# Row maxima carried inside the attention's own contraction: three bf16 rows sent by SyncE transfers in place of the pick products

## The reference, cut to what matters

```python
q = x @ wq + bq                      # (256 rows, 16 heads, 8 wide)
s = q @ q.T / sqrt(128)              # per head, 256 x 256
p = softmax(s)                       # row maximum taken off first
y = (p @ q) @ wu + bu
```

## Time and profile before

| | |
|---|---|
| three timed runs | 2505.82, 2507.54 (median), 2507.85 us |
| the profiled execution's own time | 2515.66 us |
| its span, first to last instruction | 2513.9 us |
| TensorE matmuls busy | 2036.8 us (81%) |
| VectorE busy | 1426.1 us (57%) |
| ScalarE busy | 1236.0 us (49%) |
| GpSimd busy | 648.7 us (26%) |
| mean granted TensorE clock | 0.909 |

### The profile page before, as it was taken

One profiled execution on the slowest core, in us unless ns is written; L12 is line 12 of the kernel. 1 busy time (PEld: TensorE's weight loads), 2 busy tenths in 40 slices (PEclk: granted clock), 3 DMA queues, 4 the chain that ended last, 5 costly groups with the idle time before them and its releaser, 6 DMA issues.

```text
span 2513.9 us, 38918 instructions
## 1 busy us (share of the span) xinstructions
PE 2036.8 (81%) x13610; PEld 1594.7 (63%) x13610; DVE 1426.1 (57%) x4130; ACT 1236.0 (49%) x2670; POOL 648.7 (26%) x663
## 2 busy tenths in 40 slices
PE   2766773587878888998899889989998999788884
PEld 1555552476557556875787578757875886665764
DVE  5877536453556675566556565666566356356522
ACT  3766413444446455555555564555455446335431
POOL 3111003333131133124223322332233124013052
PEclk9777885699889899999899999999999999899997
DMA  7100000112211211312132213221322312312121
GB/s 237 43 1 1 1 1 0 31 45 64 56 47 44 65 52 57 85 55 55 52 91 57 65 39 89 62 65 32 92 67 60 88 52 68 89 29 61 41 62 47
DMA packets 228948, 141.29 MB, mean 56 GB/s; under 512 B 116489, under 2 KB 206732, under 8 KB 228754
## 3 DMA queue, kind: packets, MB, share of 16 engines
q1 hardware_dynamic: 174320, 85.60, 13.4%
q0 software_dynamic: 16960, 34.74, 4.6%
q10 hardware_dynamic: 37474, 18.46, 2.6%
HBM read 82.48 MB, written 57.16 MB: 56 GB/s over the span
## 4 chain that ended last, share of the span: by engine, by line
PE 53%; DVE 24%; ACT 12%; issue 6%; DMA 2%; POOL 2%; SPq 1%; ACTq 0%; POOLq 0%; DVEq 0%
PE PS L908 17%; PE PS L876 9%; DVE AR L1085 3%; PE PS L1207 3%; PE PS L1170 3%; PE PS L1188 3%; PE PS L1433 2%; PE PS L1193 2%; ACT AR L1141 2%; DVE small L332 2%; ACT AR L837 2%; ACT AR L362 2%; DVE AR L795 2%; DVE xnT L1269 1%; PE PS L911 1%
## 5 line engine op out<-in xcount | busy, mean ns | idle before, releaser
L908 PE MATMUL PS<-AR,W 128*128 128x256 f32 x2560 | 653.0, 404 | 20.9 <-DVE AR L795 15.0
L795 DVE TENSOR_TENSOR AR<-AR,PS 128x512 f32<-128x512 f32 (+1 forms) x384 | 228.6, 597 | 653.9 <-ACT AR L837 525.8
L908 PEld LDWEIGHTS PS<-AR,W 128*128 128x128 f32 x2560 | 499.8, 204 | 92.1 <-issue 17.0
L837 ACT ACTIVATE AR<-PS 128x512 f32<-128x512 f32 (+1 forms) x384 | 201.1, 525 | 556.5 <-PE PS L908 439.1
L1085 DVE TENSOR_REDUCE AR<-PS 128x2 f32<-128x512 f32 x512 | 337.2, 688 | 160.0 <-PE PS L1170 155.6
L1141 ACT ACTIVATE AR<-PS 128x512 f32<-128x512 f32 x512 | 303.6, 600 | 236.3 <-PE PS L1193 231.9
L876 PE MATMUL PS<-AR,WO 128*128 128x256 f32 (+1 forms) x1536 | 357.7, 383 | 0.0
L876 PEld LDWEIGHTS PS<-AR,WO 128*128 128x128 f32 (+1 forms) x1536 | 295.5, 193 | 42.8
L1170 PE MATMUL PS<-AR 128*128 128x256 bf16 x1024 | 204.8, 287 | 40.4 <-DVE AR L1085 25.9
L743 POOL DMA_INDIRECT AR<-YE,gidx1c x128 | 128.8, 1007 | 379.8 <-issue 231.4
L743 POOL DMA_INDIRECT AR<-YE,gidx x128 | 128.3, 1002 | 350.9 <-ACT AR L1141 310.8
(11 more groups left out here) (359 smaller groups left out, 2771.5 us busy)
## 6 DMA issues: line engine op xcount, KB each, us to landing
AR<-XE SPq DMA_DIRECT2D x128, 128.0 KB, 2.1
YE<-AR ACTq DMA_DIRECT2D x128, 128.0 KB
AR<-QD SPq DMA_DIRECT2D x384, 32.0 KB
QD<-AR SPq DMA_DIRECT2D x8, 768.0 KB, 5.2
AR<-KD SPq DMA_DIRECT2D x64, 96.0 KB
W<-in_L_ffn_w_kernel_dram SPq DMA_DIRECT2D x2, 2560.0 KB, 13.5
OD<-AR SPq DMA_DIRECT2D x128, 36.0 KB
X<-in_L_attn_dense_dram SPq DMA_DIRECT2D x8, 512.0 KB, 4.5
```

Of the source, the lines that this page charges most:

```text
L795: ins = dve.tensor_tensor(hf[:, cols], gl[i % 2][:, cols], H[:, 2 * (i % 2) + 1, cols], ALU.mult)
L837: ins = act.activation(gl[i % 2][:, cols], H[:, 2 * (i % 2), cols], ACT.Gelu_apprx_tanh)
L908: mm = pe.matmul(H[:, b0, b * CAP:(b + 1) * CAP], w0[:, e, hb * P:(hb + 1) * P], xeT[e % 2], start=True, stop=True)
```

## The change

The three negated bf16 parts of the maxima become rows 48 to 50 of the queries' tile QA, and rows 48 to 50 of the keys' tile KA hold ones, so that the two `shifted` products add the maxima by themselves and the two pick products go. To get there: VectorE writes the parts in an order that gives each slot three neighbouring rows; TensorE transposes them with two transposes instead of one; ScalarE copies 32 rows of 256 columns to MP; SyncE then moves MP to QA with eight transfers of three rows for each piece (`shifts`), and `shifted` waits at each piece's first slot for those transfers (`a_md`). The split moves to the slot in which the piece's last maximum is taken (slots 3, 8, 16, 24, ..., 48), the transposes and the copy to two slots after it (5, 10, 18, 26, 34, 42, 50), the values product behind that. Scores run up to 16 slots ahead instead of 14. The queries' loads go from six transfers to three, two of which repeat their source rows; the queries' image is written by three transfers instead of one. GpSimd issues five transfers more, once, in the first round.

```diff
-MROWS = 3 * 2 * PB
+MROWS = KR
 def scored(i):
-    return min(NS, i + PB + 6, PB + 2 * (i + 1))
+    return min(NS, i + 2 * PB, PB + 2 * (i + 1))
+SPLIT = [slot_of(PB * (c + 2) - 1) for c in range(NPC - 1)]
+TURN = [i + 2 for i in SPLIT]
+VALUES = [TURN[0] + 2] + [i + 3 for i in TURN[1:]]
 # load_kq
-for lo, hi, a in ((0, 8, 0), (8, 16, 0), (16, 24, 0), (24, 32, 8), (32, 40, 8), (40, 48, 16)):
-    sp.dma_start(QA[c % DEPTH][lo:hi, :], qr[a:a + hi - lo, :]).then_inc(S["a_kq%d" % (c % DEPTH)], 16)
+for lo, times, part in ((0, 3, 0), (3 * AD, 2, 1)):
+    rows = qr[part * AD:(part + 1) * AD].rearrange("(o d) t -> o d t", o=1)
+    sp.dma_start(QA[c % DEPTH][lo:lo + times * AD, :], rows.broadcast_to([times, AD, 2 * QUAD])
+                 ).then_inc(S["a_kq%d" % (c % DEPTH)], 16)
+sp.dma_start(QA[c % DEPTH][5 * AD:7 * AD, :], qr[2 * AD:4 * AD, :]
+             ).then_inc(S["a_kq%d" % (c % DEPTH)], 16)
 # afront_parts
-sp.dma_start(QD.rearrange("c a p t -> p (c a) t"), QP.rearrange("p c a t -> p (c a) t")
-             ).then_inc(S["a_qd"], 16)
+for a in range(3):
+    sp.dma_start(QD[:, a].rearrange("c p t -> p c t"), QP[:, :, a, :]).then_inc(S["a_qd"], 16)
 # attend_act, turned
-act.wait_ge(S["a_mxT"], NPC * n + c + 1)
-act.copy(MP[c % 2], turned_maxima(c)).then_inc(S["a_mp"], 1)
+k = NPC * n + c
+act.wait_ge(S["a_mxT"], k + 1)
+if k >= 2:
+    act.wait_ge(S["a_md"], 16 * PB * (k - 1))
+act.copy(MP[c % 2][0:32], turned_maxima(c)[0:32]).then_inc(S["a_mp"], 1)
 # attend_pe, maxima
-pe.transpose(turned_maxima(c), MS[c % 2].rearrange("p a b -> p (a b)"),
-             identb[:, :]).then_inc(S["a_mxT"], 1)
+for q in range(2):
+    mm = pe.transpose(turned_maxima(c)[:, q * P:(q + 1) * P], MS[c % 2][:, q, :], identb[:, :])
+mm.then_inc(S["a_mxT"], 1)
 # attend_pe, shifted
+if b == 0:
+    pe.wait_ge(S["a_md"], 16 * PB * (NPC * n + c + 1))
 for h in range(2):
-    pe.matmul(o[:, h * 256:(h + 1) * 256], keys(c, P, h, b), queries(c, b), start=(h == 0),
-              stop=False, skip_group_check=True)
-if b == 0:
-    pe.wait_ge(S["a_mp"], NPC * n + c + 1)
-for q in range(2):
-    mm = pe.matmul(o.rearrange("p (h q t) -> p q h t", h=2, q=2)[:, q],
-                   pick[:, q * PB + b:q * PB + b + 1].broadcast_to([P, P]),
-                   MP[c % 2].rearrange("p (o t) -> p o t", o=1).broadcast_to([P, 2, P]),
-                   start=False, stop=True, skip_group_check=True)
+    mm = pe.matmul(o[:, h * 256:(h + 1) * 256], keys(c, P, h, b), queries(c, b), start=True, stop=True)
 mm.then_inc(S["a_slot"], 1)
 # attend_sp
+def shifts(c):
+    sp.wait_ge(S["a_mp"], NPC * n + c + 1)
+    image = QA[c % DEPTH][MROWS:MROWS + 3, :].rearrange("p (g b t) -> p b g t", g=AH, b=PB)
+    for b in range(PB):
+        sp.dma_start(image[:, b], MP[c % 2][3 * b:3 * b + 3, :].rearrange("p (g t) -> p g t", g=AH)
+                     ).then_inc(S["a_md"], 16)
+
+if n is not None:
+    shifts(0)
 for c in range(NC):
     beside(c)
     if n is None:
         continue
     for p in (2 * c, 2 * c + 1):
+        if p + 1 < NPC:
+            shifts(p + 1)
         if p + DEPTH < NPC:
             sp.wait_ge(S["a_slot"], PB * (NPC * n + p + 1))
             load_kq(sp, n, p + DEPTH)
 # round_pool, first round
+for k in range(DEPTH):
+    pool.dma_start(KA[k].rearrange("p g (s t) -> p (g s) t", t=P)[MROWS:MROWS + 3],
+                   onesb[0:3, :].rearrange("p (o t) -> p o t", o=1).broadcast_to(
+                       [3, 2 * QUAD // P, P])).then_inc(S["a_kone"], 16)
+pool.dma_start(QD[:, 3].rearrange("c (u p) t -> c u (p t)", u=AD),
+               KA[0][HALF:P].rearrange("p g t -> p (g t)")).then_inc(S["a_kone"], 16)
```

More of the change, by code:

```diff
@@ L121, in build @@
         identb = sb("identb", [P, P], BF16)
-        pick = sb("pick", [P, 2 * PB], BF16)
         join = sb("join", [P, AD], BF16)
@@ L210, in build @@
         mrest = ar.take((2 * PB,))
-        MS = [ar.take((P // (2 * PB), 2 * PB), BF16) for _ in range(2)]
-        MP = [ar.take((P,), BF16) for _ in range(2)]
+        MS = [ar.take((2, P), BF16) for _ in range(2)]
+        MP = [ar.take((2 * P,), BF16) for _ in range(2)]
         qTf = tmp[:, :, :].rearrange("p a b -> p (a b)")
@@ L1068, in turned_maxima @@
         def turned_maxima(c):
-            return side_bank(c).bitcast(BF16)[:, 0:P]
+            return side_bank(c).bitcast(BF16)
         def attend_dve(dve, n, ch, beside):
@@ L1109, in attend_dve @@
                 done = scored(i)
[L1110 to L1114, removed]
+                if i in SPLIT:
+                    split(SPLIT.index(i) + 1)
+                if i in VALUES:
+                    values(VALUES.index(i) + 1)
         def attend_act(act, n, beside, stored=None):
@@ L1143, in attend_act @@
                     out(i // 16 if i % 16 > 4 else i // 16 - 1, (i // 4 - 1) % 4)
-                if li == 5 and c + 1 < NPC:
-                    turned(c + 1)
+                if i in TURN:
+                    turned(TURN.index(i) + 1)
             if n is not None:
@@ L1150, in values @@
             def values(c):
-                pe.wait_ge(S["a_mp"], NPC * n + max(c, 1))
+                pe.wait_ge(S["a_mp"], NPC * n + c + 1)
                 for b in range(PB):
@@ L1159, in scores @@
             def scores(c, b):
+                if b == 0 and c == 0 and n == 0:
+                    pe.wait_ge(S["a_kone"], 16 * (DEPTH + 1))
                 if b == 0:
-                    pe.wait_ge(S["a_kq%d" % (c % DEPTH)], 16 * 9 * (NPC // DEPTH * n + c // DEPTH + 1))
+                    pe.wait_ge(S["a_kq%d" % (c % DEPTH)], 16 * 6 * (NPC // DEPTH * n + c // DEPTH + 1))
                 if c >= 1:
@@ L1225, in attend_pe @@
                 shifted(i)
-                if c + 1 < NPC:
-                    if li == 2:
-                        if c == 0:
-                            pe.wait_ge(S["m_ysb"], stored)
-                        values(c + 1)
-                    if li == 5:
-                        maxima(c + 1)
+                if i in TURN:
+                    if i == TURN[0]:
+                        pe.wait_ge(S["m_ysb"], stored)
+                    maxima(TURN.index(i) + 1)
+                if i in VALUES:
+                    values(VALUES.index(i) + 1)
                 if li == 5:
@@ L2115, in lights @@
                     if R.has(-1):
-                        b.put((16, lambda: hold(act, S["a_qd"], 64 * (R.g(-1) + 1))),
+                        b.put((16, lambda: hold(act, S["a_qd"], 96 * (R.g(-1) + 1))),
                               (16, lambda: hold(act, S["a_kp"], 3 * (R.g(-1) + 1))))
@@ L2503, in _ @@
             ch.step(pool.memset(zrow, 0.0))
-            ch.step(pool.memset(pick[:, :], 0.0))
             ch.step(pool.memset(anti, 0.0))
@@ L2538, in _ @@
             ch.wait()
-            ch.step(pool.tensor_tensor(pick[0:MROWS, :], identb[0:MROWS, 0:2 * PB], identb[0:MROWS, 2 * PB:4 * PB],
-                                       ALU.add))
             ch.link(pool.tensor_tensor(join[0:3 * AD, :], identb[0:3 * AD, 0:AD], identb[0:3 * AD, AD:2 * AD],
                                        ALU.add))
-            ch.step(pool.tensor_tensor(pick[0:MROWS, :], pick[0:MROWS, :], identb[0:MROWS, 4 * PB:6 * PB], ALU.add))
             ch.link(pool.tensor_tensor(join[0:3 * AD, :], join[0:3 * AD, :], identb[0:3 * AD, 2 * AD:3 * AD],
```

17 lines of the change are left out of this document (9 added, 8 removed).

## The result

| | before | after |
|---|---|---|
| timed, median (lowest to highest) | 2507.69 us (2505.82 to 2516.18) | 2819.85 us (2817.44 to 2832.11) |
| ratio, with its 95% interval | | 1.125 (1.1221 to 1.1279) |
| span of the profiled execution | 2513.9 us | 2820.0 us |
| mean granted TensorE clock | 0.909 | 0.849 |
| time at the lower clock level, by the profile's record of the clock | 461 us | 856 us |

Slower, as forecast, but by 312 us where the forecast had 61.5. The time lies outside the range (to 2660) and also beyond the dear rival (a), 2699.

What follows compares the result with a forecast made beforehand. Inside an attention three engines were taken to share the limit. Terms -38 + 60 + 10 + 13 + 12 + 2.5 + 2 = +61.5 us on 2507.5 gave 2569 us; range for 8 in 10, 2525 to 2660.

Steps and rivals of the forecast that it cites:

- (a): Rival on SyncE's row transfers: 0.81 us from start to start, 130 us more in all, 2699 us; chance 0.17.
- slot 56: Piece 7's rows queue behind SyncE's wait for scatters: 8.6 us late in seven stages, +60 us; stage 0 +10 us.
- pieces 1 to 6: Waits for rows at these pieces' first slots, mostly hidden: 1.5 us a stage, +12 us in all.
- piece 0 of stage 1: Opening of stage 1: 1.5 us from copy to products where 4.1 are needed, +2.5 us.
- Part 2: Rows through SyncE: 512 transfers, 0.34 us from start to start, landing 1.7 us; MP ready to rows ready 4.1 us.
- The clock: TensorE at the lower clock after each stage's new stall: 1.6 us lost, eight times, +13 us.
- Part 3, "hidden" loads: Queries' loads issued nine slots before the scores need them: hidden; three fewer save SyncE 1.0 us a piece.
- Part 3, the lead at 0: Scores two slots further ahead bring VectorE two maxima earlier, given back in slots 46 to 48: 0 us.
- Part 1: Pick products removed from TensorE in the attentions: -38 us, at most 57.5 us by their share of the chain.
- (b): Rival: SyncE reaches piece 7's rows before slot 56, so stalls and clock loss go, 2486 us, faster; chance 0.05.

Runs made afterwards that it cites:

- e1: The changed kernel without row transfers or waits for them, maxima not taken off, exponentials' scale 64 times smaller: 2532.7 us, ratio 1.010.
- e2: The kernel before without its pick products, maxima not taken off, exponentials' scale 64 times smaller: 2487.4 us, ratio 0.9909.
- e8: e1 with the queries loaded by six transfers as before: 2501.1 us, ratio 0.999.
- e4: The changed kernel with four rows in each row transfer instead of three, the fourth zero: 2804.5 us, ratio 1.1183.
- e9: The changed kernel with e3's order, six queries' loads, and each piece's rows by two transfers through device memory with a wait between: 2682.9 us, ratio 1.0369.
- e5: The changed kernel with four row transfers a piece instead of eight, waits' counts halved, exponentials' scale 64 times smaller: 2655.2 us, ratio 1.06.
- e3: The changed kernel with piece 7's rows issued before SyncE's wait for the scatters and the experts' opening: 2763.2 us, ratio 1.0997.
- e6: The changed kernel with the queries loaded by six transfers as before instead of three: 2795.3 us, ratio 1.1148.
- e10: e8 with scores up to 14 slots ahead, as before, instead of 16: 2564.6 us, ratio 0.9911, on another chip than e8.
- e11: The kernel of e8 timed once more, on one chip with e12: 2606.1 us, ratio 1.0045.
- e12: The kernel of e10 timed once more, on the chip of e11: 2567.1 us, ratio 0.9889.

## Why the prediction was wrong in size

The account in us, from one kernel to the next. The kernel before took 2507.7 beside after, 2509.6 beside e1 and e2 and 2504.8 beside e8; the last column takes this out, by the ratios times 2507.7:

| step | forecast | by times | from | by ratios |
|---|---|---|---|---|
| pick products go | -38 | -22 | e2 against before | -23 |
| longer lead, second transpose, new places of split and copy | +2 | +14 | e8 against e2 | +20 |
| queries' loads with repeated rows | 0 | +32 | e1 against e8 | +28 |
| rows through SyncE, with all their waits and clock | +97.5 | +287 | after against e1 | +288 |
| sum | +61.5 | +310 | | +313 |

And the waits for rows alone, as the prediction split them, with the dear price of (a), 0.81 us, beside:

| wait | forecast | at (a)'s price | measured |
|---|---|---|---|
| slot 56, eight stages | 70 | 96 | 105.4 |
| pieces 1 to 6, eight stages | 12 | 116 | 177 |
| piece 0 of stage 1 | 2.5 | 2.5 | 5.4 |

- **Part 2, the price of an issue, is the step that failed.** The sum took 0.34 us, "since the shift rows, like the loads, are written to on-chip memory in few pieces". They take 0.703, and 0.745 from start to start. The dear end of 0.768 and 0.81 was near, and MP ready to rows ready came out at 7.3 us, its end being 7.4. With the low price the forecast held five of the six waits within a stage hidden or at 0.5 us; that is where most of the miss lies, 177 us against 12. The reason given, few pieces, doesn't hold: the rows are written in 48 runs, and e4 shows that their number of rows moves the price by only 8%. What makes an issue dear stays open, as said under e9. The loads of the earlier trace rows that I stood on have long rows; the stores of L1251 there, scattered like the rows and 0.768 us each, were the nearer kin, and I gave their case 0.17. The flight was 1.7 us in the sum, and 2.0 by the section of the Trainium skill that the prediction cites, which is headed for the path of GpSimd's transfers; in stage 3 of after it is 1.9 to 2.2.
- **Even (a)'s working fell short, by 121 us.** About half of that are the first three rows of the account, which came 60 us dearer than forecast. The other half are the rows: (a) priced pieces 1 to 6 at 14.5 us a stage (its 13 and the forecast's 1.5). Stage 3 has 4.9 + 4.2 + 2.0 + 3.3 + 3.8 + 2.9 = 21.1 us, all eight 177 instead of 116. I had set the need against the gap between two events of before. With the pick products gone the slots that should cover the chain are shorter themselves: e2's attentions are 37 us shorter, so there is less to hide behind. That covers at most 37 of the 61 us; the rest stays open. Piece 5, said to have as much room as piece 3, waits 3.3 to 6.5 us.
- **The gain of a shorter slot isn't kept where a piece must wait for a chain of fixed length.** The copy comes two slots into the piece, and 7 to 8 us later (10.4 where stores stand ahead) the next piece may begin, however fast the six slots between are. That follows from the timelines and fits e5, where a shorter chain ends most waits; no run changed the slots' length alone under the rows.
- **Slot 56 was right in mechanism in all eight stages.** 8.6 us were forecast and 11.9 at the dear price; 12.3 were measured in stage 3, and 18.2 in stage 0. e3 shows the order to be its cause. The four stores ahead of the rows I had counted for pieces 3 and 5 but missed at piece 7; in stage 3 of after they don't bind, since the scatters' wait ends later, but they limited e3.
- **The clock.** I took 13 us, for one stretch of some 3 us of TensorE's work a stage. But the clock falls behind the earlier waits of a stage too. The lower level holds for 856 us instead of 461, of which the rows account for 313, since e1 has 543; in stage 3 it holds from the stall through all of the last piece. e1 and after have the same 12650 matmul instructions, and these are busy 1966.9 us in e1 and 2036.6 in after. So some 70 us, five times the 13, is the most that the lower clock can have added to TensorE's own work with the rows; no run takes it apart from the waits, so how much of it is in the 287 us stays open. (By the earlier trace rows the sum's 4.7 us at the lower level would be 5.2.) The other sentence on TensorE, matmul time down by 200 us, failed: e2 shows 87 us, and in after they are back, 2036.6 us against 2036.8, most of it by the lower clock as just said.
- **Part 3, "hidden" loads.** Inside an attention they are. But each stage's first scores, in the expert stage before, wait for piece 0's loads at once, and I had looked for the cover of pieces 4 to 7 alone. In after seven stages wait there, 30.8 us, in e6 two. The claim that SyncE saves 1.0 us a piece was wrong too: 0.1.
- **Part 3, the lead at 0.** Two maxima earlier and given back later: e8 against e2, and by ratios against e10, shows 20 us, e11 against e12 39. I had read VectorE at 91% in the same stretch and used it only against the gain of part 1.
- **Part 1** took -38 of at most 57.5. In the trace of e2 the attentions give 37, in the timed runs 22 (14 to 32). The chain's shares were a fair bound. Whether -38 was also the right size is not decided: the profiled pair says so, the timed runs don't.
- **The range.** By its own words its ends would be 2537 (all 57 us back, no clock loss) and 2634 (issues half way to the dear ones); 2525 and 2660 have no working. The measured time lies outside of both.
- **Right:** the sign, VectorE's busy time (1432 against 1426 us), that the opening of stage 1 waits (5.4 us, forecast 2.5), and (b)'s fall, as slot 56 is late in every stage.

## What to carry to other kernels

Before moving a computed operand by transfers, count issues, not bytes: eight small transfers in a row are 6 us of one sequencer here, and whatever they replaced must be worth more than that. Price a transfer by the nearest row in layout (outermost size and runs), and where two rows of the trace give prices that differ twofold, carry the dear one through the whole sum to the waits that it opens. And read an in-order stream for what it already waits on at the point where the new work is put; and for each load that changes, look at its first user, not at the typical one.

## What the runs showed of the hardware

- A transfer's issue on SyncE doesn't follow its size in these layouts: 0.703 us for 1.5 KB (3 rows of 16 runs of 32 bytes), 0.646 for 4 such rows, 0.740 for 12 KB in 384 runs of 32 bytes (e9), 0.312 for 12 KB in 24 rows written straight (e9), 0.295 for 8 rows of the queries (before), 0.695 for the same kind of rows with a repeated source (after).
- Loads that repeat their source rows take nearly as long to issue as the single ones they replace (1.9 against 2.0 us for a piece) and their data are there later: 5.5 us after the last issue instead of 2.2.
- Going out to device memory and back, with a wait in the middle, was faster than eight transfers within on-chip memory: ratio 1.0369 against 1.0891, the latter with four rows a transfer and otherwise the same order and loads.

No version that does all of the work was faster than the kernel before. e12 and e10 show what there is to win if the rows could come free and early, 1.1% and 0.9%; whether another engine's queue or engine could bring them so was not tried.
